# First self attention: another order of maxima, scores, weighted sums and the next heads' work within a pair of steps

## The chip, the cores and the metric

The kernel runs on one core of one Trainium2 chip. The metric is the device time of one execution in microseconds. The engines are named as the profile names them: PE (TensorE), PEld (its weight loads), DVE (VectorE), ACT (ScalarE), POOL (GpSimd), SP (SyncE, which issues DMAs).

## The reference, cut to what matters

Two decoder blocks follow one another on x of shape 2 x 1024 x 256. The change touches only the self attention of the first block, 16 heads of width 64, no mask:

```
h = layernorm(x, ln1_g, ln1_b)
q, k, v = h @ sa_wq, h @ sa_wk, h @ sa_wv          # 16 heads of 64 each
attn = softmax(q k^T * 64 ** -0.5)                 # per batch and head, 1024 x 1024
x = concat(attn @ v) @ sa_wo + sa_bo + x
```

Cross attention, a gated feed-forward, and a second block (causal self attention, cross attention, feed-forward) follow. They are left as they are.

## The kernel before, in words

`wide_attention` (called once, with the name `sa`) works through 16 **items**: 8 pairs of heads (g), and for each the two batches (b), in the order (0,0), (0,1), (1,0) and so on. `walk` writes items of g = 0 and g = 7 out and loops over g = 1 to 6. Each item has 16 **steps**: two halves of 512 queries, in each 8 tiles of 128 keys. Two steps make a **unit** (u = 0 to 7), and per unit every engine does the following, in program order on its own queue:

- PE, a step's *scores* (L976): for both heads three products (hi x hi, hi x lo, lo x hi) of keys and queries, 64 rows of the array for each head, added onto a PSUM tile of 128 x 1024 that holds minus the row maxima already. PE, a step's *weighted* sum (L991): exponentials times values, 64 columns of the array for each head, into `out`.
- ACT: `exponent` (L1051) of a step's scores into one of four buffers `p_buf`; `seed` (L1061), the copy of the maxima into the score tile just freed, for the step two later. There are two score tiles.
- POOL: `acc` plus exponentials (L1229), for the denominators.

Beside this runs the *front* work, mostly for the next item, as listed by unit in the table `lanes` (`lanes_first` for item 0; "c" is work of the item itself, "n" of the next, "p" of the one before):

- q or k, of 512 tokens (L920, six products): ACT `high` (L1044) copies the rounded part out, then DVE `low` (L1130) the rest, and with that the bank is free.
- v (L930, 16 products): DVE copies it out (L1140).
- m, maxima (L939): the scores of 128 queries and 512 keys of both heads, in one bank for each head; DVE reduces each (L1146). Sixteen m per item.
- t, twice per item: when 8 m of a half are reduced, DVE joins them (L1161), PE turns the result (L944), DVE drains it (L1154), and SP sends it through DRAM into `m_all` (L866, L868), which `seed` of step 0 or 8 waits for.
- den, twice per item: PE sums `acc` over partitions (L951), ACT `take_sums` (L1074) frees the bank, and DVE inverts it in four pieces (L1168, `invert`, two pieces per unit).

All front work goes through **three PSUM banks** in turn: `places` numbers the uses in the table's order, an m taking two, and PE's `wait_free` waits before a use until the use three before it is drained. DVE drains in the table's order, and counts all drains on one semaphore.

On PE a unit is issued by `both` (L1001 on): a leading t if there is one, the first m, scores of step 2u, the second m, scores of step 2u+1, a third m, then the rest (`behind`), then the weighted sums of steps 2u-2 and 2u-1. On ACT: both exponentials, a seed, the high part or `take_sums`, a seed. On DVE: the maxima, the pieces to invert (previous item's second half in u = 2, 3, this one's first half in u = 6, 7), then q, k, v and t.

Of the kernel before, what the change touches and what calls it, by code (L numbers as in the profile page):

```python
# [643 lines left out]
def wide_attention(nc, name, hT, ident, ones, w, oT, spare):  # L644
# [17 lines left out]

    lanes = {
# [8 lines left out]
    }  # L672
    lanes_first = {
# [6 lines left out]
        6: lanes[6],  # L680
        7: lanes[7],
    }
# [7 lines left out]
    def lanes_of(g, b):  # L690

        return lanes_first if isinstance(g, int) and (g, b) == (0, 0) else lanes
# [49 lines left out]
    def is_first(g, b):  # L742
        return isinstance(g, int) and (g, b) == (0, 0)

    def is_last(g, b):
        return isinstance(g, int) and (g, b) == (NG - 1, 1)
# [5 lines left out]
    def before(g, b):  # L752
        return (g, 0) if b == 1 else (g - 1, 1)

    def after(g, b):
        return (g, 1) if b == 0 else (g + 1, 0)

    def owner(who, g, b):

        if who == "c":  # L760
            return g, b
        if who == "p":
            return None if is_first(g, b) else before(g, b)
        return None if is_last(g, b) else after(g, b)

    def owned(u, g, b, kinds):

        return [(owner(who, g, b), item) for who, item in lanes_of(g, b)[u]
                if item[0] in kinds and owner(who, g, b) is not None]

    def behind(u, g, b):

        kinds = ("q", "k", "v", "den")
        return owned(u, g, b, kinds if leads(u, g, b) else kinds + ("t",))

    def leads(u, g, b):

        return owned(u, g, b, ("t",)) if lanes_of(g, b)[u][0][1][0] == "t" else []

    def sums(s):  # L780

# [13 lines left out]
    with ExitStack() as ctx:  # L795
# [58 lines left out]
        with nc.Block() as block:  # L854
# [37 lines left out]
            def _(pe):  # L892
# [107 lines left out]

                def both(g, b):  # L1001
                    for u in range(UNITS):
                        for of, item in leads(u, g, b):
                            front_item(*of, item)
                        tops = owned(u, g, b, "m")
                        for of, item in tops[:1]:
                            front_item(*of, item)
                        scores(g, b, 2 * u)
                        for of, item in tops[1:2]:
                            front_item(*of, item)  # L1010
                        scores(g, b, 2 * u + 1)
                        for of, item in tops[2:]:
                            front_item(*of, item)
                        for of, item in behind(u, g, b):
                            front_item(*of, item)
                        if u >= 1:
                            weighted(g, b, 2 * u - 2)
                            weighted(g, b, 2 * u - 1)
                        elif not is_first(g, b):
                            weighted(*before(g, b), STEPS - 2)  # L1020
                            weighted(*before(g, b), STEPS - 1)
                    if is_last(g, b):
                        weighted(g, b, STEPS - 2)
                        weighted(g, b, STEPS - 1)
                        wait_free(g, b, ("den", 1))
                        denominators(g, b, ("den", 1))
# [4 lines left out]
            def _(act):  # L1031
# [55 lines left out]
                def both(g, b):  # L1087
                    for u in range(UNITS):
                        if u == 1 and not is_first(g, b):
                            take(*before(g, b), 1)  # L1090
                        if u == UNITS // 2 + 1:
                            take(g, b, 0)
                        exponent(g, b, 2 * u)
                        exponent(g, b, 2 * u + 1)
                        if u < UNITS - 1:
                            coming = [(g, b, 2 * u + 2), (g, b, 2 * u + 3)]
                        elif not is_last(g, b):
                            coming = [(*after(g, b), 0), (*after(g, b), 1)]
                        else:
                            coming = []  # L1100
                        for n in coming[:1]:
                            seed(*n)
                        for of, item in owned(u, g, b, ("q", "k", "den")):
                            if item[0] == "den":
                                take_sums(*of, item[1])
                            else:
                                high(*of, item)
                        for n in coming[1:]:
                            seed(*n)
                        if u == UNITS - 2 and splits(g, b):  # L1110
                            split_w(g + 1)
                    if is_last(g, b):
                        take(g, b, 1)
                        take_sums(g, b, 1)
# [4 lines left out]
            def _(dve):  # L1119
# [55 lines left out]

                def both(g, b):
                    for u in range(UNITS):
                        for of, item in leads(u, g, b) + owned(u, g, b, "m"):
                            front_item(*of, item)
                        if u in (2, 3) and not is_first(g, b):  # L1180
                            invert(*before(g, b), 1, 2 * u - 4)
                            invert(*before(g, b), 1, 2 * u - 3)
                        if u in (6, 7):
                            invert(g, b, 0, 2 * u - 12)
                            invert(g, b, 0, 2 * u - 11)
                        for of, item in behind(u, g, b):
                            if item[0] != "den":
                                front_item(*of, item)
                    if is_last(g, b):
                        for piece in range(4):  # L1190
                            invert(g, b, 1, piece)
# [1027 lines left out]
```

## Time and profile before

| | |
|---|---|
| median of 3 runs | 1942.18 us (1940.86 to 1942.22) |
| profiled execution, its own time | 1953.28 us |
| its span, first to last instruction | 1951.6 us |
| busy over the span: PE, DVE, ACT, POOL | 90%, 58%, 52%, 47% |
| this stage's 256 exponentials start from / to | 75.2 to 820.0 us |
| from an item's first exponential to the next item's: first, then the others | 56.3, then 46.9 to 47.1 us (median 46.93) |

The stage that is changed fills about 750 of the 1951.6 us of the span. In a timeline row stand start and length in us, engine, line, operation, tiles, shapes and the count of merged instructions; brackets hold idle time of the engine before it and what ended it. The matmuls' ends are modelled in this profile and overlap the next one's start, so distances between starts say more than lengths.

### The profile page before, as it was taken

The page shows a single profiled execution, that of the slowest core. Times are in us where ns is not written, and L with a number is a line of the kernel's source. Part 1 is how long each engine was busy: PE and PEld are TensorE (multiplying, and loading weights), DVE is VectorE, ACT ScalarE, POOL GpSimd, SP SyncE. Part 2 cuts the span into 40 slices and gives each one's busy share as a digit, 9 for nine tenths or more (in the row PEclk, how much of TensorE's full clock was granted, in tenths as well). Part 3 has the DMA queues.
Part 4 walks back from the last instruction along what each step waited for, and adds up shares of the span by engine and source line. Part 5 has one row for each costly group of instructions (what it writes and reads, how often), then busy time and mean ns, then how long its engine had stood idle before and what let it go on. Part 6 is the DMA issues. An engine that isn't in the chain of part 4 may idle for free. (4 is left out here: it accounts for less than half of the span.)

```text
span 1951.6 us, 28723 instructions
## 1 busy us (share of the span) xinstructions
PE 1754.6 (90%) x9620; PEld 1071.5 (55%) x9620; DVE 1138.0 (58%) x2069; ACT 1007.6 (52%) x1312; POOL 922.3 (47%) x806
## 2 busy tenths in 40 slices
PE   4689999999999999889999989995999886898799
PEld 2344454455444444366555868883444435565678
DVE  4556666666666666334666343446688834787501
ACT  3367777777777777712444132310566671454440
POOL 1267777777777777920222200201355663466010
PEclk9899999999999999989999989995799998999899
DMA  1000000000000000040000010103344410000101
GB/s 54 25 28 28 25 28 24 27 24 27 24 27 24 27 24 26 19 121 25 1 1 1 1 41 24 27 11 61 61 78 84 77 36 23 9 1 1 33 18 40
DMA packets 53918, 60.30 MB, mean 31 GB/s; under 512 B 18560, under 2 KB 44444, under 8 KB 53823
## 3 DMA queue, kind: packets, MB, share of 16 engines
q1 hardware_dynamic: 49471, 52.50, 10.6%
q0 software_dynamic: 4352, 6.56, 1.6%
q8 instruction: 56, 0.92, 0.2%
q14 instruction: 39, 0.32, 0.1%
HBM read 39.62 MB, written 2.37 MB: 22 GB/s over the span
## 5 line engine op out<-in xcount | busy, mean ns | idle before, releaser
L1229 POOL TENSOR_TENSOR x<-x,sa_p_buf 128x1024 f32<-128x1024 f32 x192 | 456.5, 2378 | 136.9 <-ACT sa_p_buf L1051 126.0
L1146 DVE TENSOR_REDUCE sa_mx<-sa_front 128x1 f32<-128x512 f32 x512 | 328.8, 686 | 100.7 <-PE sa_front L939 98.1
L1051 ACT ACTIVATE sa_p_buf<-sa_score 128x1024 f32<-128x1024 f32 x256 | 260.0, 1026 | 156.7 <-PE sa_score L976 156.2
L1061 ACT ACTIVATE sa_score<-sa_m_all 128x1024 f32<-128x1024 f32 x256 | 258.5, 1025 | 9.0 <-DMA sa_m_all<-sa_m_line 9.0
L991 PE MATMUL sa_out<-sa_p_buf,sa_v_buf 128*64 128x512 f32 x1024 | 246.1, 602 | 0.0
L528 ACT ACTIVATE sa_p_buf<-sa_score 128x1024 f32<-128x1024 f32 (+1 forms) x160 | 141.1, 938 | 88.8 <-PE sa_score L476 88.7
L1721 POOL TENSOR_TENSOR x<-x,bias_out 128x1024 f32<-128x1024 f32 x24 | 55.7, 2349 | 269.3 <-POOLq L1906 151.9
L342 DVE TENSOR_REDUCE sa_mx<-sa_front 128x1 f32<-128x512 f32 (+1 forms) x256 | 156.0, 651 | 27.8 <-PE sa_front L283 24.9
L939 PE MATMUL sa_front<-sa_k_hi,sa_q_hi 64*128 64x512 f32 x512 | 130.1, 505 | 23.3 <-DVE sa_mx L1146 9.8
L939 PEld LDWEIGHTS sa_front<-sa_k_hi,sa_q_hi 64*128 64x128 f32 x512 | 48.5, 186 | 168.2 <-DVE sa_mx L1146 74.7
L1610 POOL TENSOR_TENSOR ca_probs<-ca_s_sb,ca_inv 128x616 f32<-128x616 f32 x64 | 77.9, 1218 | 127.6 <-DVE ca_inv L1544 127.6
L991 PEld LDWEIGHTS sa_out<-sa_p_buf,sa_v_buf 128*64 128x64 f32 x1024 | 64.9, 136 | 118.9 <-issue 87.7
L1168 DVE RECIPROCAL x<-x 128x128 f32<-128x128 f32 x128 | 111.9, 918 | 29.4 <-ACT x L1074 29.4
L283 PE MATMUL sa_front<-sa_k_top,sa_q_top 59*128 59x128 f32 (+4 forms) x576 | 87.9, 373 | 40.2 <-DVE sa_mx L342 29.6
L580 POOL TENSOR_SCALAR_AFFINE_SELECT sa_p_buf<-sa_p_buf 128x128 f32<-128x128 f32 x256 | 65.1, 292 | 98.7 <-ACT sa_p_buf L528 98.6
L283 PEld LDWEIGHTS sa_front<-sa_k_top,sa_q_top 33*128 33x128 f32 (+1 forms) x576 | 54.4, 210 | 103.5 <-DVE sa_mx L342 83.5
L1739 PE MATMUL po_prod<-w_out,o 128*128 128x256 f32 x384 | 91.0, 396 | 21.3 <-PEq L415 11.6
L1229 POOL TENSOR_TENSOR x<-sa_p_buf 128x1024 f32<-128x1024 f32 x32 | 75.8, 2370 | 68.2 <-ACT sa_p_buf L1051 68.2
L976 PE MATMUL sa_score<-sa_q_hi,sa_k_hi 64*128 64x512 f32 x512 | 104.9, 405 | 3.0 <-ACT sa_score L1061 2.9
L1467 ACT ACTIVATE ca_turned<-ca_t_ps 128x1024 f32<-128x1024 f32 x64 | 65.5, 1024 | 77.7 <-PE ca_t_ps L1413 77.7
L976 PE MATMUL sa_score<-sa_q_hi,sa_k_lo 64*128 64x512 f32 x512 | 101.8, 393 | 0.0
L976 PE MATMUL sa_score<-sa_q_lo,sa_k_hi 64*128 64x512 f32 x512 | 101.5, 392 | 0.0
(185 smaller groups left out, 3277.9 us busy)
## 6 DMA issues: line engine op xcount, KB each, us to landing
sa_m_all<-sa_m_line SPq DMA_DIRECT2D x32, 512.0 KB, 3.6
x<-in_x SPq DMA_DIRECT2D x8, 512.0 KB, 7.4
sa_q_stack<-sa_hi SPq DMA_DIRECT2D x64, 64.0 KB, 2.3
sa_k_stack<-sa_hi SPq DMA_DIRECT2D x64, 64.0 KB, 2.4
ff_w<-in_L_xattn_ff_w SPq DMA_DIRECT2D x16, 128.0 KB, 2.2
sa_k_top<-sa_hi POOLq DMA_DIRECT2D x32, 64.0 KB, 2.7
sa_q_top<-sa_hi POOLq DMA_DIRECT2D x32, 64.0 KB, 2.6
sa_q_stack<-sa_lo SPq DMA_DIRECT2D x32, 64.0 KB, 2.4
```

Of the source, the lines that this page charges most:

```text
L283: mm = pe.matmul(bank(i, item, u)[:, c0 + lo_k:c0 + hi_k], q_top[base:base + rows_of, b, r, at], k_top[base:base + rows_of, b, r, k0 + lo_ ...
L342: dve.tensor_reduce(mx[:, b, j, place:place + 1], fr[u][:, 0:n], AX.X, ALU.max).then_inc(drained, 1)
L528: nc.scalar.activation(p_buf[:, n % NPB, 2 * r:2 * r + 2, 0:cols], score_ps[r][:, :, 0:cols], ACT.Exp, scale=SCALE).then_inc(exp_done, 1)
L939: pe.matmul(front_ps[bank(item, j)][:], q_hi[r, b, qt * P:(qt + 1) * P], k_hi[r, b, half * HALF:(half + 1) * HALF], start=True, stop=True) ...
L976: mm = pe.matmul(score_ps[s % len(score_ps)][:, j, :], ks[r, b, keys], qs[r, b, queries], start=False, stop=(part == 2), skip_group_check= ...
L991: mm = pe.matmul(out_ps[64 * j:64 * j + 64, :], v_buf[:, b, kt, 64 * j:64 * j + 64], p_buf[:, s % NPB, j, :], start=(kt == 0), stop=(kt == ...
L1051: nc.scalar.activation(p_buf[:, s % NPB], score_ps[s % len(score_ps)][:], ACT.Exp, scale=SCALE).then_inc(exp_done, G)
L1061: nc.scalar.activation(score_ps[s % len(score_ps)][:], m_all[:, h, :].rearrange("p (j n) -> p j n", j=G), ACT.Identity).then_inc(seeded, G)
L1146: dve.tensor_reduce(mx[:, b, j, qt, half:half + 1], front_ps[bank(item, j)][:], AX.X, ALU.max).then_inc(drained, 1)
L1168: dve.reciprocal(recip[:, h, at], recip[:, h, at]).then_inc(inverted, 1)
L1229: nc.gpsimd.tensor_tensor(acc[:, h], prev, cur, ALU.add).then_inc(added, 1)
L1739: mm = pe.matmul(prod[i % NPROD][:, t, :], src[:, k, at:at + P], wt[:, k, :], start=(k == 0), stop=(k == KN - 1))
```

## The change

`lanes` and `lanes_first` move some entries within a unit; `leads`, `behind` and `owned` by kinds are replaced by `leading` (all entries up to the first m) and `trailing` (the rest). PE issues the leading entries, both steps' scores, then a second m (and den 0, in unit 5), then the two weighted sums, then the rest. ACT does both seeds ahead of the high part, and takes den 0 ahead of both. DVE keeps the table's order of drains, and inverts this item's first half in units 5 and 6 in place of 6 and 7.

```diff
     lanes = {
-        1: [("c", ("m", 7, 1)), ("c", ("t", 1)), ("n", ("q", 0)), ("p", ("den", 1))],
+        1: [("c", ("m", 7, 1)), ("n", ("q", 0)), ("c", ("t", 1)), ("p", ("den", 1))],
...
-        7: [("n", ("m", 6, 0)), ("n", ("m", 7, 0)), ("n", ("m", 4, 1)), ("n", ("v", 1))],
+        7: [("n", ("m", 6, 0)), ("n", ("m", 7, 0)), ("n", ("v", 1)), ("n", ("m", 4, 1))],
     lanes_first = {
-        1: [("c", ("m", 6, 0)), ("c", ("m", 7, 0)), ("c", ("m", 4, 1)), ("n", ("q", 0))],
-        2: [("c", ("m", 5, 1)), ("c", ("m", 6, 1)), ("c", ("m", 7, 1)), ("n", ("k", 1))],
+        1: [("c", ("m", 6, 0)), ("c", ("m", 7, 0)), ("n", ("q", 0)), ("c", ("m", 4, 1))],
+        2: [("c", ("m", 5, 1)), ("c", ("m", 6, 1)), ("n", ("k", 1)), ("c", ("m", 7, 1))],
...
-        4: [("n", ("m", 2, 0)), ("n", ("m", 3, 0)), ("n", ("m", 0, 1)), ("n", ("v", 0))],
-        5: [("n", ("m", 1, 1)), ("n", ("m", 2, 1)), ("n", ("m", 3, 1)), ("c", ("den", 0))],
+        4: [("n", ("m", 2, 0)), ("n", ("m", 3, 0)), ("n", ("v", 0)), ("n", ("m", 0, 1))],
+        5: [("n", ("m", 1, 1)), ("n", ("m", 2, 1)), ("c", ("den", 0)), ("n", ("m", 3, 1))],
...
+    def owned(u, g, b):
+        return [(owner(who, g, b), item) for who, item in lanes_of(g, b)[u] if owner(who, g, b) is not None]
+    def leading(u, g, b):
+        table = lanes_of(g, b)[u]
+        first = [item[0] for _, item in table].index("m") + 1
+        return [x for x in owned(u, g, b) if x[1] in [item for _, item in table[:first]]]
+    def trailing(u, g, b):
+        return owned(u, g, b)[len(leading(u, g, b)):]
...
# PE
                     for u in range(UNITS):
-                        for of, item in leads(u, g, b):
-                            front_item(*of, item)
-                        tops = owned(u, g, b, "m")
-                        for of, item in tops[:1]:
+                        for of, item in leading(u, g, b):
                             front_item(*of, item)
                         scores(g, b, 2 * u)
-                        for of, item in tops[1:2]:
-                            front_item(*of, item)
                         scores(g, b, 2 * u + 1)
-                        for of, item in tops[2:]:
-                            front_item(*of, item)
-                        for of, item in behind(u, g, b):
+                        behind = trailing(u, g, b)
+                        cut = sum(1 for n, x in enumerate(behind) if (n, x[1][0]) == (0, "m") or x[1] == ("den", 0))
+                        for of, item in behind[:cut]:
                             front_item(*of, item)
                         if u >= 1:
                             weighted(g, b, 2 * u - 2)
...
                             weighted(*before(g, b), STEPS - 1)
+                        for of, item in behind[cut:]:
+                            front_item(*of, item)
# ACT
-                        for n in coming[:1]:
+                        if u == 5:
+                            take_sums(g, b, 0)
+                        for n in coming:
                             seed(*n)
-                        for of, item in owned(u, g, b, ("q", "k", "den")):
-                            if item[0] == "den":
-                                take_sums(*of, item[1])
+                        for of, item in owned(u, g, b):
+                            if item == ("den", 1):
+                                take_sums(*of, 1)
                             else:
                                 high(*of, item)
-                        for n in coming[1:]:
-                            seed(*n)
# DVE
-                        for of, item in leads(u, g, b) + owned(u, g, b, "m"):
+                        mine = [x for x in owned(u, g, b) if x[1][0] != "den"]
+                        cut = len(mine) if u == 7 else sum(1 for x in mine if x[1][0] not in ("q", "k", "v"))
+                        for of, item in mine[:cut]:
                             front_item(*of, item)
...
-                        if u in (6, 7):
-                            invert(g, b, 0, 2 * u - 12)
-                            invert(g, b, 0, 2 * u - 11)
-                        for of, item in behind(u, g, b):
-                            if item[0] != "den":
-                                front_item(*of, item)
+                        if u in (5, 6):
+                            invert(g, b, 0, 2 * u - 10)
+                            invert(g, b, 0, 2 * u - 9)
+                        for of, item in mine[cut:]:
+                            front_item(*of, item)
```

No operation is added or removed, and no tile or DMA changes. `places` follows the tables, so the numbers of the banks change with them.

## Rows read from the trace of the kernel before

**Rows 1.** Windows of first, eighth and last item; columns name themselves
```profile
72.80:129.10 56.30, 46.38 (x250) 24.09 (x252) 33.44 (x54) 36.98 (x41) 31.27 (x14) 0.97 0.06 20
...
413.60:460.50 46.90, 46.06 (x260) 23.40 (x258) 32.09 (x51) 35.41 (x41) 36.85 (x18) 1.00 0.08 28
788.00:835.00 47.00, 36.06 (x187) 13.46 (x183) 14.46 (x20) 31.85 (x36) 38.11 (x19) 0.91 0.04 12
```

**Rows 2.** Timeline of PE, unit 3 of the eighth item
```profile
430.19 0.50 PE L939 MATMUL sa_front<-sa_k_hi,sa_q_hi 64*128 64x512 f32 x2
...
431.47 0.50 PE L939 MATMUL sa_front<-sa_k_hi,sa_q_hi 64*128 64x512 f32 x2
...
432.27 0.40 PE L976 MATMUL sa_score<-sa_q_hi,sa_k_lo 64*128 64x512 f32 x2
432.59 0.51 PE L920 MATMUL sa_front<-sa_h_hi,sa_w_hi 128*128 128x512 f32 x1
...
433.86 0.39 PE L920 MATMUL sa_front<-sa_h_hi,sa_w_lo 128*128 128x512 f32 x1
434.18 1.94 PE L991 MATMUL sa_out<-sa_p_buf,sa_v_buf 128*64 128x512 f32 x8
436.05 0.51 PE L939 MATMUL sa_front<-sa_k_hi,sa_q_hi 64*128 64x512 f32 x2
```

**Rows 3.** Timelines of ACT and DVE, the same unit 3
```profile
431.53 1.03 ACT L1051 ACTIVATE sa_p_buf<-sa_score 128x1024 f32<-128x1024 f32 x1 [1.22 <-PE sa_score L976]
...
434.69 0.59 ACT L1044 ACTIVATE sa_q_hi<-sa_front 128x512 fp32r<-128x512 f32 x1
...
430.73 2.56 DVE L1146 TENSOR_REDUCE sa_mx<-sa_front 128x1 f32<-128x512 f32 x4 [0.61 <-PE sa_front L939]
...
435.31 0.69 DVE L1130 TENSOR_TENSOR sa_q_lo<-sa_front,sa_q_hi 128x512 fp32r<-128x512 f32 x1 [0.35 <-ACT sa_q_hi L1044]
```

**Rows 4.** Timeline of PE, first item: maxima straight behind scores
```profile
73.40 0.40 PE L976 MATMUL sa_score<-sa_q_hi,sa_k_lo 64*128 64x512 f32 x2
73.64 0.40 PE L939 MATMUL sa_front<-sa_k_hi,sa_q_hi 64*128 64x512 f32 x2
```

**Rows 5.** Timeline of PE, unit 1 of the eighth item
```profile
417.85 0.50 PE L939 MATMUL sa_front<-sa_k_hi,sa_q_hi 64*128 64x512 f32 x2
...
419.92 0.27 PE L944 MATMUL sa_front<-ident,sa_m_row 128*8 128x128 f32 x1 [0.20 <-DVE sa_m_row L1161]
420.01 0.49 PE L920 MATMUL sa_front<-sa_h_hi,sa_w_hi 128*128 128x512 f32 x1
...
421.59 1.08 PE L951 MATMUL sa_front<-x,ones 128*64 128x512 f32 x4
422.50 1.89 PE L991 MATMUL sa_out<-sa_p_buf,sa_v_buf 128*64 128x512 f32 x8
424.31 0.50 PE L939 MATMUL sa_front<-sa_k_hi,sa_q_hi 64*128 64x512 f32 x2
```

**Rows 6.** Timeline of PE, end of unit 7
```profile
454.47 0.50 PE L939 MATMUL sa_front<-sa_k_hi,sa_q_hi 64*128 64x512 f32 x2
455.07 2.05 PE L930 MATMUL sa_front<-sa_wv,hT 128*128 128x128 f32 x16
457.05 1.94 PE L991 MATMUL sa_out<-sa_p_buf,sa_v_buf 128*64 128x512 f32 x8
```

**Rows 7.** Timeline of DVE, unit 6: drain of turned maxima
```profile
447.75 0.28 DVE L1154 TENSOR_SCALAR sa_m_turned<-sa_front 8x128 f32<-8x128 f32 x1 [2.14 <-PE sa_front L944]
```

**Rows 8.** Timeline of DVE, unit 7: the copy of values
```profile
457.88 0.63 DVE L1140 COPY sa_v_buf<-sa_front 128x512 f32<-128x512 f32 x1
```

**Rows 9.** Timelines of PE and ACT, first item
```profile
102.77 0.63 PE L939 MATMUL sa_front<-sa_k_hi,sa_q_hi 64*128 64x512 f32 x2 [2.20 <-DVE sa_q_lo L1130]
...
100.45 1.03 ACT L1061 ACTIVATE sa_score<-sa_m_all 128x1024 f32<-128x1024 f32 x1 [2.90 <-DMA sa_m_all<-sa_m_line]
```

**Rows 10.** Window of the first item with the low clock
```profile
102.00:107.00 5.00, 4.12 (x18) 2.47 (x18) 3.27 (x5) 2.40 (x3) 0.00 (x0) 0.66 0.00 0
```

More of the change, by code:

```diff
@@ L764, in owner @@
         return None if is_last(g, b) else after(g, b)
[L766 to L778, printed above, removed]
+    def owned(u, g, b):
[6 more added lines that the diff above has]
+        return owned(u, g, b)[len(leading(u, g, b)):]
     def sums(s):
```

## The prediction

> **What bounds the kernel now.** I read the windows first, then the timeline of PE between the starts of its instructions, then ACT and DVE beside it. In a steady item PE is busy 46.06 of 46.90 us at the full clock (1.00, 2.4 GHz), while DVE has 32, ACT 35 and POOL 37 us [rows 1]. So PE sets the time of the 14 middle items, of 46.93 us each. But busy is not streaming. In unit 3 a matmul of 512 columns follows its like after 0.23 us: five of them from 432.59 to 433.86 are 1.27, the first 0.10 longer [rows 2]. A pair of maxima is thus 0.23 of streaming, a step's scores 0.69, q or k 1.37, two weighted sums 1.72 of the 1.87 from 434.18 to 436.05. That makes 4.92 of the unit's 5.86 us (430.19 to 436.05). The other 0.94 lies between kinds:
> - where the form of the array changes (64 rows, full, 64 columns), a gap of 0.09 to 0.10 (433.86 to 434.18 is 0.32 instead of 0.23; 432.27 to 432.59 as well) and then a weight load that nothing covers, 0.10 for 128 columns, 0.05 for 64;
> - before the second maxima: scores end at 430.19+0.33+0.69 = 431.21, the maxima start at 431.47. DVE's four reductions take 0.64 each [rows 3]; the first began at 430.73 and ended at 431.42, and frees the bank. 0.25 of wait, and 0.10 of weights.
>
> Scores to maxima with a free bank is 73.40 to 73.64, 0.24 us: no gap, weights hidden [rows 4].
>
> **The working.** The sum comes from a walk by these rows: PE, ACT, DVE and POOL go through all 16 items in program order, each operation starting when its queue and what it waits for allow, with these durations and the bank order of `places`. For the old order this gives units 0 to 7 of 5.82, 6.41, 5.82, 5.82, 6.22, 5.29, 4.40, 6.96, sum 46.75 against 46.93 in the trace, and 55.3 against 56.3 for the first item. Delays between engines come from rows: DVE starts 0.20 after the end of a stream (430.52 to 430.73), ACT 0.30 (431.21 to 431.53) [rows 2, 3].
>
> **Gains, per steady item.** In a usual unit the old changes cost 0.20 + 0.35 + 0.19 + 0.14 = 0.88 (weighted to maxima, scores to maxima, scores to q, q to weighted). The new ones cost 0.14 (maxima to weighted) + 0.20 (weighted to q) + 0.19 (q to maxima) + 0 = 0.53. That is 0.36 saved in units 0, 2, 3, 4 and 5, and 0.31 in unit 6. Unit 1 saves only 0.1: the turn t waits 0.3 less for the join (419.92 [rows 5] against a scores' end at 419.55), but has one change of form more. Unit 7 saves 0.87: two waits of 0.35, and m to v which takes 0.60 instead of 0.33 [rows 6]. Sum 3.1 us, if nothing new were late.
>
> **What is late next.** The q, k or v now stands directly ahead of the next unit's maxima; before, 1.87 us of weighted sums stood between them while ACT and DVE drained it. DVE drains in order, so the next reductions wait behind it, and with three banks the second maxima need the first one's bank.
> - Units 3 and 4, after k or q. Count from the end of the projection's stream. ACT starts the high part at 0.29 and takes 0.59, DVE the low part at 0.93, 0.69 [rows 3]; the first reduction runs from 1.58 to 2.27, and PE may go at 2.33. PE is there at 0.09+0.10+0.23+1.37 = 1.80. Wait 0.53, exposed weights 0.10: 0.63 each, 1.27 together. In unit 1 there is no second maxima. Unit 2 escapes only since the next wait comes before it.
> - Unit 1 to 2. In the table t now stands behind q. DVE can drain t only after q's low part, at 1.58, in 0.28 [rows 7]. The maxima of unit 2 take t's bank: 1.92 at the earliest. PE (t 0.09, den 0.91 [rows 5], gaps) is there at 1.18. Wait 0.74.
> - Unit 7 to 0. m(4,1) now follows v(1) directly, and m(5,1) follows m(4,1), which needs m(4,1)'s bank. DVE copies v from 0.20 to 0.83 [rows 8], reduces until 1.51, PE may go at 1.57; it is there at 0.42. Wait 1.15 and weights 0.10, 1.25. In the old order v's 1.98 and the weighted sums' 1.87 lay between these two maxima [rows 6].
> - Small: den 0 waits 0.09 for its bank; unit 6 shrinks to 4.1, and ACT's two exponentials and two seeds (four times 0.95) hold step 15 for 0.22; m(7,0) loses 0.10. Together 0.4.
>
> Sum 3.7 us of new waits against 3.1 gained: +0.56 per item, 47.3 against 46.75 in the same walk, +7.8 for 14 items. The earlier `invert` and `take_sums` in unit 5 cost nothing: DVE has 0.3 of the item idle, which covers them; without it they would add to the DVE chains above. Both seeds ahead of the high part cost nothing in a steady item, as the high part now waits for its projection 0.3 to 1.2 us anyway.
>
> **First and last item.** The first has 8 more maxima and is bound by DVE's drains already: 56.30 us with PE at 46.4 busy [rows 1]. In `lanes_first` q(0) and k(1) now stand inside the maxima, so that m(4,1) and m(7,1) wait 1.6 us each for a high and low part that had been behind them, and t(1) stands directly behind m(7,1): 1.7 us for two reductions and the join. The maxima of step 8 then arrive late in `m_all`. Already now ACT waits 2.90 us for them, the high part of q(1) behind that, and PE 2.20 for the low part [rows 9]; new, q's high part stands behind two seeds, one more second. Walk: 61.5 against 55.3, +6.2. Bounds 3 (half of these waits hidden by one another) and 10 (each with the low clock: the granted clock fell to 0.66 over 102 to 107 us [rows 10], 3.4 us at the 1.2 GHz level, right after PE's long wait, and a second such stretch costs another 1.7). The last item has no projections, ACT's 35 us hardly wait; walk -0.4.
>
> **Sum.** +7.8 + 6.2 - 0.4 = +13.6. On the profiled execution (1953.28, span 1951.6) 1966.9; this execution lies 11.1 above the median, the difference is laid on the median: 1942.2 + 13.6 = 1955.8, say 1956.
>
> **A rule weighed.** The rows show the weights of the maxima loaded under the scores, in the same rows of the array [rows 4]. The Trainium skill, TensorE: Matmul & The Clock Gate, section The mechanism, says that a weight load overlaps matmuls in flight only when their row groups differ. By it the second maxima would show 0.10 in the four units where no wait shows it yet, 0.4 per item, and the time would be 1962. The trace speaks against it.
>
> **The rivals.**
> - *Faster: the new waits are smaller than the gains.* The point is 1.0 us per item (0.56, and the first item's 6.2 over 14). The one place is unit 7 to 0: were the 1.25 there hidden, items would take 46.06, -0.7 each, -10 in 14, +5.8 outside: 1938. For it speaks only that unseen sequences may overlap better than the walk has them; against it that old units come out within 0.13 us. Chance 0.08.
> - *No change.* The 0.56 is 1.2% of an item, the walk missed the old item by 0.4%. Were each of the four large waits 0.15 shorter (ACT and DVE starting sooner than 0.29 and 0.20), steady items tie, and with the low bound of the first item the time is 1945, within reach of the old. Chance 0.10.
> - *Much slower, by the first item and the clock.* More and longer waits of PE bring the low clock two or three times more, also into the second item; +9 of waits, +5 of clock, +9 steady: 1965. For: [rows 10]; against: steady items keep 1.00 through idle of 0.5, the new waits are up to 1.25. Chance 0.08.
> - *The page's rule above*, 1962 by an uncovered 0.10 at each second maxima. Chance 0.02.
>
> **The numbers.** My forecast keeps 0.72. A measurement of this kernel can tell 0.2%, 3.9 us. Faster 0.08, same 0.10, slower 0.72+0.08+0.02 = 0.82. Range: low is +0.1 per item and +2 in the first, 1945; high is +1.0 per item (waits 0.1 longer each) and the first item's 10, 1966. It leaves out the faster rival and little above.
>
> **What would show it.** In the profile after: scores of a unit x12 without a gap and maxima 0.24 behind the last (right step 1); units 0 and 2 at 5.45; units 3 and 4 at 6.1 and 6.5 with PEld waiting for DVE's reduction at the second maxima; unit 1 at 7.05, ended by DVE's drain of t; unit 7 at 7.7 with the wait of 1.2 between L939 and L939. The distance of exponentials 16 apart at 47.4 to 47.6. A distance under 46.9 makes the prediction wrong; so does a first item under 58.

## The result, and the profile after

The kernel after takes 1952.55 us (median of 20 runs, 1946.81 to 1963.77), the one before 1945.04 us (20 runs, 1940.34 to 1955.66). The ratio is 1.0036, 95% interval 1.0021 to 1.0051: slower by 7.5 us by the medians, where 1956 and +13.6 were forecast. The direction held, but the sum behind it has most of the loss in the wrong items.

The windows of the first and of the eighth item of the kernel after, as in [rows 1]:

```profile
74.50:137.80 63.30, 48.93 (x256) 26.08 (x254) 33.73 (x55) 36.34 (x41) 31.99 (x14) 0.92 0.04 17
419.00:465.90 46.90, 45.08 (x259) 23.78 (x258) 31.45 (x50) 35.07 (x40) 36.83 (x18) 1.00 0.10 31
```

The eighth item, from its first exponential to the next item's, in the timeline of ACT:

```profile
421.76 1.03 ACT L1048 ACTIVATE sa_p_buf<-sa_score 128x1024 f32<-128x1024 f32 x1 [3.57 <-PE sa_score L976]
...
468.68 1.03 ACT L1048 ACTIVATE sa_p_buf<-sa_score 128x1024 f32<-128x1024 f32 x1 [3.75 <-PE sa_score L976]
```

468.68 - 421.76 = 46.92 us, against 46.93 before. The 14 middle items together take 657.0 us after and 657.5 before: **a tie**. The first takes 63.3 us (56.3 before), with the granted clock at 0.92 over it (0.97 in [rows 1]). The last takes 30.8 us to its last exponential (31.0 before).

The tie of the middle items is a sum of gains and losses, though. From exponential 2u to 2u+2, in us:

| unit | 0 | 1 | 2 | 3 | 4 | 5 | 6 | 7 | sum |
|---|---|---|---|---|---|---|---|---|---|
| before | 5.86 | 6.47 | 5.89 | 5.86 | 6.26 | 5.32 | 4.36 | 6.91 | 46.93 |
| forecast after | 5.45 | 7.05 | 5.45 | 6.09 | 6.49 | 5.02 | 4.09 | 7.66 | 47.3 |
| after | 5.50 | 6.95 | 5.49 | 5.98 | 6.35 | 5.05 | 4.00 | 7.60 | 46.92 |

The row "forecast after" puts the prediction's gains and waits onto the units of its walk for the old order (unit 5 is 5.29 - 0.36 + 0.09). Every unit is within 0.15 us of it. Units 0, 2, 5 and 6 are shorter than before by 1.4 us together, units 1, 3, 4 and 7 longer by as much. The timeline of PE around a k (it answers to [rows 2]), with ACT and DVE beside it:

```profile
438.05 0.39 PE L920 MATMUL sa_front<-sa_h_hi,sa_w_lo 128*128 128x512 f32 x1
438.37 0.50 PE L939 MATMUL sa_front<-sa_k_hi,sa_q_hi 64*128 64x512 f32 x2
438.70 0.40 PE L976 MATMUL sa_score<-sa_q_hi,sa_k_hi 64*128 64x512 f32 x2
...
439.86 0.40 PE L976 MATMUL sa_score<-sa_q_hi,sa_k_lo 64*128 64x512 f32 x2
440.45 0.50 PE L939 MATMUL sa_front<-sa_k_hi,sa_q_hi 64*128 64x512 f32 x2 [0.19 <-DVE sa_mx L1143]
440.88 1.94 PE L991 MATMUL sa_out<-sa_p_buf,sa_v_buf 128*64 128x512 f32 x8
442.75 0.50 PE L920 MATMUL sa_front<-sa_h_hi,sa_w_hi 128*128 128x512 f32 x1
...
438.48 0.60 ACT L1041 ACTIVATE sa_k_hi<-sa_front 128x512 fp32r<-128x512 f32 x1 [0.47 <-PE sa_front L920]
...
439.11 0.69 DVE L1127 TENSOR_TENSOR sa_k_lo<-sa_front,sa_k_hi 128x512 fp32r<-128x512 f32 x1 [1.12 <-ACT sa_k_hi L1041]
439.72 2.56 DVE L1143 TENSOR_REDUCE sa_mx<-sa_front 128x1 f32<-128x512 f32 x4
```

The last product of k starts at 438.05, so its stream ends at 438.28. ACT takes it at 438.48, DVE at 439.11, and the next reduction can start only at 439.72. It is over 0.69 later (the length of one in [rows 3]'s four), at 440.41, and the second maxima start at 440.45. The scores ended at 439.86 + 0.23 = 440.09. So PE waits 0.36 us for the bank.

The turn of unit 1 to 2 (it answers to [rows 5]) and the end of unit 7 (it answers to [rows 6]), timeline of PE:

```profile
431.12 0.27 PE L944 MATMUL sa_front<-ident,sa_m_row 128*8 128x128 f32 x1
431.33 1.08 PE L951 MATMUL sa_front<-x,ones 128*64 128x512 f32 x4
432.89 0.50 PE L939 MATMUL sa_front<-sa_k_hi,sa_q_hi 64*128 64x512 f32 x2 [0.48 <-DVE sa_m_turned L1151]
```

From den to the maxima is 1.56 us, where its 0.86 of streaming and a gap would make 0.96. PE waits 0.60, for the drain of t, which stands behind q's low part.

```profile
418.99 0.51 PE L939 MATMUL sa_front<-sa_k_hi,sa_q_hi 64*128 64x512 f32 x2
420.44 0.50 PE L939 MATMUL sa_front<-sa_k_hi,sa_q_hi 64*128 64x512 f32 x2 [0.94 <-DVE sa_mx L1143]
420.78 0.39 PE L976 MATMUL sa_score<-sa_q_hi,sa_k_hi 64*128 64x512 f32 x2
```

These are the end of unit 7 and the start of the eighth item's unit 0. The maxima m(4,1) start at 418.99 and their stream ends at 419.32, m(5,1) starts at 420.44. This wait is 1.12 us, for m(4,1)'s own reduction behind the copy of v.

### The profile page after: what moved, and what is told of

Its sections match the earlier page's. It is cut to its first block and busy times, and to the rows that moved or that the text cites. A ratio compares the mean times of both kernels' runs of the same rounds, so it can differ in the third digit from the quotient of the medians.

```text
span 1950.7 us, 28729 instructions
## 1 busy us (share of the span) xinstructions
PE 1736.9 (89%) x9620; PEld 1076.3 (55%) x9620; DVE 1126.0 (58%) x2069; ACT 1001.5 (51%) x1312; POOL 923.6 (47%) x806
## 3 DMA queue, kind: packets, MB, share of 16 engines
q0 software_dynamic: 4352, 6.56, 1.7%
## 5 line engine op out<-in xcount | busy, mean ns | idle before, releaser
L1048 ACT ACTIVATE sa_p_buf<-sa_score 128x1024 f32<-128x1024 f32 x256 | 248.9, 1023 | 149.1 <-PE sa_score L976 147.2
L1058 ACT ACTIVATE sa_score<-sa_m_all 128x1024 f32<-128x1024 f32 x256 | 253.0, 1032 | 6.7 <-DMA sa_m_all<-sa_m_line 6.7
L939 PE MATMUL sa_front<-sa_k_hi,sa_q_hi 64*128 64x512 f32 x512 | 122.4, 474 | 43.1 <-DVE sa_mx L1143 29.5
```

What stands on the lines that cost most here:

```text
L939: pe.matmul(front_ps[bank(item, j)][:], q_hi[r, b, qt * P:(qt + 1) * P], k_hi[r, b, half * HALF:(half + 1) * HALF], start=True, stop=True) ...
L1048: nc.scalar.activation(p_buf[:, s % NPB], score_ps[s % len(score_ps)][:], ACT.Exp, scale=SCALE).then_inc(exp_done, G)
L1058: nc.scalar.activation(score_ps[s % len(score_ps)][:], m_all[:, h, :].rearrange("p (j n) -> p j n", j=G), ACT.Identity).then_inc(seeded, G)
```

## The experiments

Two theories stood after this. **Banks:** gains and waits for the three banks cancel in a steady item by chance, and each can be removed by itself. **Another bound:** both kernels come out at 46.93 because something else (POOL's or ACT's chain) holds an item there; then removing a wait does nothing. The kernel before ran beside each set (medians 1945 to 1947 us). A kernel's difference to the one before is taken between medians of the same set (for the kernel after it is +7.5), and two kernels of different sets are compared by these differences. Differences of middle items come from the profiles, which repeat to 0.1 us.

### e1_seven: v ahead of unit 0 again

```diff
-        7: [..., ("n", ("m", 7, 0)), ("n", ("v", 1)), ("n", ("m", 4, 1))],
+        7: [..., ("n", ("m", 7, 0)), ("n", ("m", 4, 1)), ("n", ("v", 1))],
```

> The kernel after, with unit 7 of lanes put back to m(6,0), m(7,0), m(4,1), v(1), so that v again stands between m(4,1) and the next unit's m(5,1). Theory (gains and new waits on the three banks cancel by chance in a steady item): the wait of 1.12 us and the uncovered weights go, a steady item falls from 46.93 to about 45.9, unit 7 from 7.5 to about 6.5; the whole is 14 us under the kernel after, about 7 under the one before. Rival (something else, POOL's or ACT's chain, holds the item at 46.93 in both kernels): the item stays at 46.9 and the time within 2 us of the kernel after.

Measured: 1936.75 us, ratio to before 0.9962 (0.9941 to 0.9982). Timeline of PE, end of unit 7, and of ACT at both ends of this item:

```profile
410.58 0.50 PE L939 MATMUL sa_front<-sa_k_hi,sa_q_hi 64*128 64x512 f32 x2
411.01 2.05 PE L930 MATMUL sa_front<-sa_wv,hT 128*128 128x128 f32 x16
412.99 0.50 PE L939 MATMUL sa_front<-sa_k_hi,sa_q_hi 64*128 64x512 f32 x2
...
414.31 1.03 ACT L1048 ACTIVATE sa_p_buf<-sa_score 128x1024 f32<-128x1024 f32 x1 [2.55 <-PE sa_score L976]
...
460.21 1.03 ACT L1048 ACTIVATE sa_p_buf<-sa_score 128x1024 f32<-128x1024 f32 x1 [2.72 <-PE sa_score L976]
```

The maxima at 412.99 come 1.98 us after the start of v, v's own length: no wait is left. The item is 45.90 us, 1.02 shorter, and unit 7 has 6.56. Fourteen of them are 14 us; the kernel is 9.8 us under the one before, and with the 7.5 that makes 17 under the one after. One edit in a table turns the slower kernel into one slightly faster than before (0.4%); "another bound" falls.

### e2_first: q, k and v of the first item behind its maxima again

```diff
     lanes_first = {
-        1: [m(6,0), m(7,0), q(0), m(4,1)],
-        2: [m(5,1), m(6,1), k(1), m(7,1)],
-        4: [m(2,0), m(3,0), v(0), m(0,1)],
+        1: [m(6,0), m(7,0), m(4,1), q(0)],
+        2: [m(5,1), m(6,1), m(7,1), k(1)],
+        4: [m(2,0), m(3,0), m(0,1), v(0)],
```

> The kernel after, with units 1, 2 and 4 of lanes_first put back (q(0), k(1) and v(0) behind all maxima of their unit). Theory, that the first item's 7 us come from maxima waiting for a projection's drain: the walk gives 60.2 in place of 61.1 for the first item, so only 1 us back, because the third maxima then wait for one another; steady items unchanged; 1 us under the kernel after. Rival (the whole of the 7 us sits in these three table rows): the first item back at 56 to 57, 6 to 7 us under the kernel after.

Measured: 1948.33 us, ratio 1.0018 (1.0000 to 1.0037); the first item 59.97 us instead of 63.31, the others unchanged (46.93). Both expectations miss: 3.3 us come back in the profile, not 1 and not 7. Its first item has 3.4 us at the 1.2 GHz level, that of the kernel after 10.2. An estimate, which is used again below, charges at most half the length of such a stretch to the clock, as PE runs at 1.2 in place of 2.4 GHz in it: up to 3.4 us here, so that little or nothing is left for the order of the table. By medians the kernel is 1.7 us over the one before, 5.8 less than the kernel after, and the two intervals overlap. So what these three rows are worth stays open.

### e3_cover: the weighted sums last again

```diff
-                        cut = sum(1 for n, x in enumerate(behind) if (n, x[1][0]) == (0, "m") or x[1] == ("den", 0))
+                        cut = len(behind)
```

> The kernel after with one edit: on PE the weighted sums come last in the unit, behind q, k, v and the rest of the table's row, as they did before the change; both scores stay together. Theory: all gains stay, and the weighted sums again cover the drain of q, k and v: a steady item at 45.1, units of 5.5, 6.7, 5.5, 5.7, 5.9, 5.0, 4.1, 6.8; the first item 59; the whole about 28 us under the kernel after and 20 under the one before. Rival (another bound at 46.93 per item): within 2 us of the kernel after.

Measured: 1920.95 us, ratio 0.9866 (0.9837 to 0.9896). Timeline of PE around a k, and of ACT at both ends of the eighth item:

```profile
426.20 0.39 PE L976 MATMUL sa_score<-sa_q_hi,sa_k_lo 64*128 64x512 f32 x2
426.43 0.40 PE L939 MATMUL sa_front<-sa_k_hi,sa_q_hi 64*128 64x512 f32 x2
426.83 0.50 PE L920 MATMUL sa_front<-sa_h_hi,sa_w_hi 128*128 128x512 f32 x1
...
428.41 1.94 PE L991 MATMUL sa_out<-sa_p_buf,sa_v_buf 128*64 128x512 f32 x8
430.27 0.51 PE L939 MATMUL sa_front<-sa_k_hi,sa_q_hi 64*128 64x512 f32 x2
430.62 0.40 PE L976 MATMUL sa_score<-sa_q_hi,sa_k_hi 64*128 64x512 f32 x2
...
408.44 1.03 ACT L1048 ACTIVATE sa_p_buf<-sa_score 128x1024 f32<-128x1024 f32 x1 [2.56 <-PE sa_score L976]
...
453.12 1.03 ACT L1048 ACTIVATE sa_p_buf<-sa_score 128x1024 f32<-128x1024 f32 x1 [2.73 <-PE sa_score L976]
```

The second maxima start 0.23 after the last product of the scores: weights hidden, no wait. Then k (426.83 to 428.41) and 1.86 of weighted sums, under which ACT and DVE drain k, and the next maxima at 430.27 find their banks free. An item is 44.68 us, 2.2 under both kernels, and the kernel 25.6 us under the one before (20 were expected). This is what the change would have brought with this one line different.

### e4_seed_high_seed: the high part between the seeds

In unit 5 `take_sums` stays ahead of both seeds, as in the kernel after.

```diff
-                        for n in coming:
+                        for n in coming[:1]:
                             seed(*n)
...                             high(*of, item)
+                        for n in coming[1:]:
+                            seed(*n)
```

> The kernel after with ACT's old order: one seed, the high part, the second seed. Theory: the high part now waits for a projection that PE issues behind the weighted sums, and the second seed waits behind it, so step 2u+3 starts late: a steady item at 49.3 (+2.4), the whole about 33 us over the kernel after. Rival (the ACT order is of no weight, the seeds have slack): within 2 us of the kernel after.

Measured: 1975.82 us, ratio 1.0145 (1.0108 to 1.0181); an item 48.5 us (+1.6; +2.4 had been expected), the whole 29 us over the kernel before. Timeline of ACT, then of PE, at the end of a unit 0:

```profile
430.76 1.04 ACT L1058 ACTIVATE sa_score<-sa_m_all 128x1024 f32<-128x1024 f32 x1
433.23 0.60 ACT L1041 ACTIVATE sa_k_hi<-sa_front 128x512 fp32r<-128x512 f32 x1 [1.44 <-PE sa_front L920]
433.73 1.02 ACT L1058 ACTIVATE sa_score<-sa_m_all 128x1024 f32<-128x1024 f32 x1
...
433.93 0.40 PE L976 MATMUL sa_score<-sa_q_hi,sa_k_lo 64*128 64x512 f32 x2
434.80 0.50 PE L976 MATMUL sa_score<-sa_q_hi,sa_k_hi 64*128 64x512 f32 x2 [0.48 <-ACT sa_score L1058]
```

ACT has nothing to do for 1.4 us, until k is there at 433.23, and the second seed stands behind it. PE's second scores wait until 434.80 instead of 434.16. So with the projection moved behind the weighted sums, both seeds ahead of the high part are needed.

### e5_old_fills_first: both seeds first, in the old PE order

The kernel before, with both seeds ahead of the high part and of `take_sums`. This is not quite ACT's part of the change, which takes den 0 ahead of both seeds in unit 5:

```diff
-                        for n in coming[:1]:
+                        for n in coming:
                             seed(*n)
...                             high(*of, item)
-                        for n in coming[1:]:
-                            seed(*n)
```

> The kernel before with one part of the change alone, ACT's: both seeds ahead of the high part and of take_sums. Theory: with q and k still ahead of the weighted sums, their drain is a second of ACT later, and the next maxima wait for it: a steady item at 48.6 (+1.7), the whole 25 us over the kernel before. Rival (seeds earlier are a gain by themselves): the item at or under 46.9.

Measured: 1970.87 us, ratio 1.0145 (1.0103 to 1.0187), a middle item 48.46 us (+1.5; +1.7 had been expected). Against the kernel before, units 1, 3 and 4 are 0.24 us longer each and unit 5 is 0.8 longer. Timeline of ACT, then of PE, at the turn from unit 5 to 6:

```profile
456.40 1.97 ACT L1061 ACTIVATE sa_score<-sa_m_all 128x1024 f32<-128x1024 f32 x2
458.30 0.59 ACT L1074 ACTIVATE x<-sa_front 128x512 f32<-128x512 f32 x1
...
459.01 0.50 PE L939 MATMUL sa_front<-sa_k_hi,sa_q_hi 64*128 64x512 f32 x2 [0.73 <-ACT x L1074]
```

The 0.8 of unit 5 is den 0's bank, which `take_sums` frees one seed later. The change doesn't have this cost, so the run shows 0.7 us per item for q and k behind both seeds in the old PE order, and not 1.5 for ACT's part of the change. That part by itself was not run.

### e7_scores_only: PE's scores together, nothing else

```diff
                         scores(g, b, 2 * u)
-                        for of, item in tops[1:2]:
-                            front_item(*of, item)
                         scores(g, b, 2 * u + 1)
-                        for of, item in tops[2:]:
+                        for of, item in tops[1:]:
                             front_item(*of, item)
```

> The kernel before with one part of the change alone, on PE: both steps' scores back to back, the second maxima behind them; tables, ACT and DVE as before. Theory: the two gains (no wait for the bank at the second maxima, its weights hidden) come with this edit alone, less a longer unit 7: a steady item at 45.4, units of 5.5, 6.4, 5.5, 5.5, 5.9, 4.9, 4.1, 7.8, the whole 18 us under the kernel before. Rival (the gain needs the other parts too): the item at 46.9 or more.

Measured: 1924.54 us, ratio 0.9898 (0.9864 to 0.9932); a middle item 45.43 us, units of 5.5, 6.5, 5.5, 5.5, 5.9, 5.0, 4.0, 7.6. The gains of the forecast (no wait for the bank, hidden weights) come with this edit; the whole is 20.5 us under the kernel before (18 were expected). What spent them in the change is the weighted sums moved forward. The entries moved in the table are a gain once the weighted sums stay last: in e3 above and e9 below, with v ahead of m(4,1), unit 7 is 6.6 us in place of the 7.6 here.

### e8_cover_first_as_before: e3 with the old first item

The old `lanes_first`, and for the first item alone a maxima between the scores and one seed behind the high part:

```diff
+                        behind = trailing(u, g, b)
                         scores(g, b, 2 * u)
+                        if is_first(g, b):
+                            front_item(*behind[0][0], behind[0][1])
+                            behind = behind[1:]
                         scores(g, b, 2 * u + 1)
-                        behind = trailing(u, g, b)
...
+                        late = 1 if is_first(g, b) else 2
-                        for n in coming:
+                        for n in coming[:late]:
                             seed(*n)
...                             high(*of, item)
+                        for n in coming[late:]:
+                            seed(*n)
```

> e3_cover with the first item as in the kernel before (its table, a maxima between the two scores, seed, high part, seed). Theory, that the first item's loss comes from its order alone: the first item back from 64.5 to about 57, steady items at 44.7; 6 to 8 us under e3_cover, the fastest so far. Rival (the first item's loss lies in the low clock or the DMA of the maxima whatever the order): within 2 us of e3_cover.

Measured: 1917.20 us, ratio 0.9864 (0.9832 to 0.9895), 27.9 us under the kernel before where e3 is 25.6 under; the intervals do not tell the two apart, and the 6 to 8 us expected are not seen. In the profile the first item takes 58.9 us instead of 64.5, the middle ones 44.72. The first item has 6.8 us of low clock and e3's 13.6, which by the estimate of e2 is up to 3.4 of the 5.6 us.

### e9_cover_seed_high_seed: e3 with the old order of ACT

Both edits together, `cut = len(behind)` of e3 and the seed, high part, seed of e4 (den 0 in unit 5 still ahead of both seeds).

> e3_cover with ACT's old order: seed, high part, seed. Theory: with q and k ahead of the weighted sums again, the high part is not late, and the order of ACT costs and gains nothing: a steady item at 44.8, within 2 us of e3_cover; units 1, 3 shorter, unit 6 longer. Rival (seed, high part, seed costs by itself, as in e4_seed_high_seed): over 20 us more.

Measured: 1906.97 us, ratio 0.9807 (0.9777 to 0.9838), **the fastest**. It is 38.1 us under the kernel before, 12.5 more than e3, where 2 at most were expected. A middle item takes 44.18 us, 0.5 less than in e3: unit 1 is 6.23 instead of 6.60, units 3 and 4 0.09 shorter each, as q and k are rounded one seed earlier (in e3 the maxima of unit 2 wait for the drain of t behind q, with 0.30 us of PE idle, and here they don't wait); unit 6, which the walk had made longer, stayed at 4.0. That is 7.4 us in 14 items. The first item takes 57.05 instead of 64.45, the other 7.4. Windows of the first item, of e3, then of e9:

```profile
75.00:139.00 64.00, 48.84 (x246) 25.77 (x244) 33.56 (x54) 34.98 (x40) 32.20 (x15) 0.89 0.06 19
```

```profile
75.00:132.00 57.00, 44.10 (x250) 23.24 (x250) 33.89 (x55) 34.93 (x40) 32.81 (x15) 1.00 0.07 22
```

The clock column is 0.89 in e3 and 1.00 in e9: e3 has two stretches of 6.8 us at the 1.2 GHz level, e9 none. Half of 13.6 us is 6.8, so the clock can be nearly all of the first item's 7.4. One profiled execution of each kernel can't show that ACT's order kept the clock up.

### e10_first_as_before, e12_first_again, e13_after_again: is the loss the first item's alone?

e10 and e12 are the kernel after with e8's edit of the first item, and for the others the `cut` of the change:

```diff
-                        cut = sum(1 for n, x in enumerate(behind) if (n, x[1][0]) == (0, "m") or x[1] == ("den", 0))
+                        cut = len(behind) if is_first(g, b) else sum(
+                            1 for n, x in enumerate(behind) if (n, x[1][0]) == (0, "m") or x[1] == ("den", 0))
```

e13 is the kernel after, unchanged.

> The kernel after with the first item alone put back: its table, a maxima between the two scores, weighted sums last, seed, high part, seed. All other items as in the kernel after. Theory (steady items tie, so the whole loss of 7 us is the first item's): the first item at 57, steady items at 46.93, the whole within 2 us of the kernel before. Rival (part of the loss lies elsewhere, in later stages or in the last item): 4 us or more over the kernel before.

> The same kernel as e10_first_as_before, whose twelve times fell in two groups (1944.0 to 1949.4 and 1953.8 to 1958.8). Theory (the first item's loss is the whole; the upper group comes from a longer low-clock stretch in a later stage, as in the profiled execution of the kernel before): most times in the lower group, median within 4 us of the kernel before. Rival (a loss of some 7 us that is not in the first item): median 6 us or more over the kernel before again.

> The kernel after itself, beside e12 on one chip. Theory: 7 us over the kernel before, and over e12 by 4 to 7 us. Rival: level with e12.

Measured: e10 1951.59 us, ratio 1.0031 (1.0011 to 1.0051); the same kernel again 1949.45 us, 1.0023 (0.9999 to 1.0047); the kernel after again 1952.90 us, 1.0045 (1.0029 to 1.0060). By medians the old first item gives back 3.5 us of some 7.6 (e13 against e12, where 4 to 7 were expected); e10 was expected within 2 us of the kernel before and is 6.6 over it, as its rival had it; e12 is 4.1 over, between its theory (4) and its rival (6). The ratios leave the rest unclear. The profiles of e10 and e12 have first items of 58.9 and 60.1 us, not 56.3, e13's 62.1. The middle items take 656.9 and 657.0 us. Unit 1 took 11.4 us in e10 and 7.2 in the kernel before. Timelines of PE in unit 1, behind its scores, of the kernel before, then of e10:

```profile
81.23 0.50 PE L939 MATMUL sa_front<-sa_k_hi,sa_q_hi 64*128 64x512 f32 x2
81.83 0.50 PE L920 MATMUL sa_front<-sa_h_hi,sa_w_hi 128*128 128x512 f32 x1
```

```profile
81.92 0.50 PE L939 MATMUL sa_front<-sa_k_hi,sa_q_hi 64*128 64x512 f32 x2 [0.68 <-DVE sa_mx L1150]
83.21 0.79 PE L920 MATMUL sa_front<-sa_h_hi,sa_w_hi 128*128 128x512 f32 x1 [0.78 <-DVE sa_mx L1150]
```

Every engine's order is that of the kernel before up to unit 4, but the banks are not. `places` numbers banks from `lanes` for all items, the first too, and a use waits for the last use of the same bank. So in the first item a wait can reach back one or two uses, not always three, and v ahead of m(4,1) in `lanes` moves m(4,1) of the first item onto the two banks that m(7,0) has just filled. That puts m(4,1) 0.6 us later and q(0) 1.3 us later in e10 than in the kernel before (with the 0.1 by which e10 starts later taken off). Behind it comes a low-clock stretch of 6.8 us from 82.5 us on; the kernel before has one of 3.4 us, at 103 us. So e8, e10, e11 and e12 don't restore the old first item, and no run with the new `lanes` does.

### e11_best: e9 with the old first item

e9 with e8's table and PE order for the first item.

> e9_cover_seed_high_seed with the first item's table and PE order as in the kernel before. Theory: steady items at 44.2 as in e9, the first item at 56.3 in place of 57.1, the whole 1 us under e9: no difference that can be told. Rival (the low clock after the first item's waits comes back with this order, as in the kernel before): 2 us over e9.

Measured: 1914.75 us (four runs, 1908.59 to 1916.53), ratio 0.9851 (0.9833 to 0.9870). It is 30.2 us under the kernel before where e9 is 38.1, so 8 us slower than e9; 1 us faster was expected, and 2 us slower by the rival. The profiled execution has low-clock stretches of 6.8 and 3.4 us in the first item (59.4 us), none in e9's (57.05). Middle items take 44.17 us, as in e9. The rival's direction and cause fit; its size does not.

## Why the prediction was right, and where it was not

**Right, by the mechanism:** PE sets the time. The scores run without a gap and the second maxima start 0.23 after them with hidden weights (e3, e7). The projection without cover makes the next second maxima wait (units 3 and 4), the drain of t makes the maxima of unit 2 wait, v holds m(5,1). The earlier inversions cost nothing that shows: unit 5 is 4.96 to 4.98 us in e3, with them, and in e7, without.

**The term that failed is the +0.56 per steady item; it measured 0.0.** The gains were right where a unit shows them alone (units 0 and 2 forecast at 5.45, measured 5.50 and 5.49). The waits of the sum were too large: those in units 3 and 4 are 0.36 instead of 0.53, the one behind t 0.60 instead of 0.74, and only the largest, 1.12 for 1.15, was right. With 0.10 of weights in three places that is 2.7 us, and with the small terms of 0.4, which were not measured one by one, 3.1: as much as was gained. Half of the error of units 3 and 4 is ACT's start. The forecast has the high part 0.29 after the projection's stream, the distance of an exponential behind scores; it measured 0.20 (438.28 to 438.48). The trace of the kernel before had the right pair, in the first item (timelines of PE and ACT):

```profile
83.09 0.40 PE L920 MATMUL sa_front<-sa_h_hi,sa_w_lo 128*128 128x512 f32 x1
...
83.52 0.60 ACT L1044 ACTIVATE sa_q_hi<-sa_front 128x512 fp32r<-128x512 f32 x1 [0.30 <-PE sa_front L920]
```

Its stream ends at 83.09 + 0.23 = 83.32, 0.20 ahead of ACT. The rest is small: the reduction follows the low part by 0.61, not 0.65, and PE the reduction by 0.04, not 0.06. A difference of two sums of 3 us each was off by 0.56, and 14 items multiplied it to 8. The prediction's own sign, exponentials 47.4 to 47.6 us apart, was missed (46.92), and "under 46.9" was escaped by 0.02.

**The first item** was forecast at +6.2 and measured +7.0, and +5.7 in e13, the same kernel. That this came so near is in part luck, for the walk knows no clock. The kernel after has stretches of 3.4 and 6.8 us at the 1.2 GHz level, at 88.7 and 99.0 us, e13 one of 6.8, the kernel before one of 3.4. With half of these taken off (the estimate of e2, the most that the clock can be) 58.2 and 58.7 us stand against 54.6: order and banks are worth 4 us or somewhat more, not 6.2, and up to 3.4 of the 7.0 are clock. Four waits of PE and ACT in the kernel after:

```profile
87.96 0.50 PE L939 MATMUL sa_front<-sa_k_hi,sa_q_hi 64*128 64x512 f32 x2 [1.42 <-DVE sa_q_lo L1127]
...
97.55 0.50 PE L939 MATMUL sa_front<-sa_k_hi,sa_q_hi 64*128 64x512 f32 x2 [1.41 <-DVE sa_k_lo L1127]
...
105.67 1.97 ACT L1058 ACTIVATE sa_score<-sa_m_all 128x1024 f32<-128x1024 f32 x2 [0.54 <-DMA sa_m_all<-sa_m_line]
...
109.97 0.50 PE L939 MATMUL sa_front<-sa_k_hi,sa_q_hi 64*128 64x512 f32 x2 [1.41 <-DVE sa_q_lo L1127]
```

m(4,1) and m(7,1) wait for a low part, as forecast (1.6 us each). But the waits around step 8 were to grow and shrank: ACT waits 0.54 us for `m_all` instead of 2.90, and PE 1.41 for q(1)'s low part instead of 2.20 [rows 9]. Unit 5, which the forecast for the first item does not name, is 2.2 us longer than before (8.92 for 6.68). The first item also has five maxima more than a middle one by the tables, not eight: eight of its own where a middle one has three. The last item: -0.4 forecast, -0.2 measured.

So the direction rests on the first item alone, and its number on a sum that was too large and a clock that was not in it.

**The rivals.** "Faster" named the right place: e1 shows that without the wait of unit 7 to 0 the kernel is 0.4% under the one before. It needed an edit of the table. "No change" had the right mechanism for the middle items, waits 0.15 shorter than in the sum, and that is what three of the four were. The page's rule on weight loads (the Trainium skill, TensorE: Matmul & The Clock Gate, section The mechanism: overlap only when row groups differ) is contradicted by the maxima 0.23 us behind the scores at 426.20 and 426.43 in e3: same row groups, same spacing as within the scores. The loads of both heads' weights start at 426.23, while the scores' last products run (timeline of PEld):

```profile
426.23 0.19 PEld L939 LDWEIGHTS sa_front<-sa_k_hi,sa_q_hi 64*128 64x128 f32 x2
```

The same section also lets a load go ahead into a background buffer of weights; no row names that buffer.

## What to carry to other kernels

When a queue of few buffers is drained through two engines, put the longest work that needs none of them (here the weighted sums) right behind the item with the longest drain. Moving it away left nothing of a gain of some 3 us per item; putting it back (one line) made the kernel 1.3% faster than before, and with the old order of ACT 1.9%. Change one queue's order at a time: the scores together on PE alone brought 1.0%, both seeds first on ACT alone cost 1.5%. Where a table also numbers the buffers, an entry moved for one item changes the waits of the others. And where a forecast is the difference of two sums, measure each start delay for its own pair of engines and shapes.

## What the runs showed of the hardware that was not expected

The same instruction stream gives different low-clock stretches from one execution to the next. The kernel after has 3.4 and 6.8 us of them in its first item and, as e13, 6.8; one kernel had 6.8 us as e10 (first item 58.9 us) and 3.4 and 6.8 as e12 (60.1). A later stage, which no edit touches, does the same. Windows of the second block's attention, of the kernel before, then of the kernel after:

```profile
1323.10:1620.40 297.30, 239.21 (x1832) 121.04 (x1832) 204.63 (x383) 159.10 (x201) 141.55 (x384) 0.86 0.36 65
```

```profile
1332.50:1622.00 289.50, 230.84 (x1832) 116.88 (x1832) 204.47 (x383) 158.81 (x202) 142.19 (x384) 0.90 0.38 67
```

Both windows run from the stage's first maxima to the first product behind it: the same work, 297.3 us and 289.5 us, at a granted clock (third column from the right) of 0.86 and 0.90. One stretch at 1.2 GHz there lasts 64.9 us in the one and 47.8 in the other. That is most of the 8 us by which the profiled execution of the kernel before (1953.28 us) lies over its median of 1945; e13's has it too (61.4 us). By the clock column the windows have some 83 and 58 us at the low level in all. The 7.8 us are a third of that difference, less than the half that the estimate of e2 takes as the most. So the two profiled spans, 1951.6 and 1950.7 us, hide the loss: up to the end of the changed stage the kernel after is 8 us behind (7.0 of the first item, 1.7 ahead of its first exponential, less 0.7), behind it 9 us ahead. No row says why a stretch is long.
